# Perceiver block on one core: when GpSimd splits the queries' weights, and ScalarE's order beside it

## What is computed

```python
def _layernorm(x, axis=-1, eps=1e-05):
    m = jnp.mean(x, axis=axis, keepdims=True)
    v = jnp.var(x, axis=axis, keepdims=True)
    return (x - m) / jnp.sqrt(v + eps)
...
x = x + xattn(layernorm(x), ctx_768, w_q, w_k, w_v, w_o, b_o)     # x: 64*32 rows x 512
#   q = x @ w_q (512 x 1024), k = ctx @ w_k, v = ctx @ w_v, 16 heads of 64
#   softmax(q k' / 8) v, then @ w_o + b_o
x = x + attn(layernorm(x), w_attn, w_proj, decay_raw)              # 16 heads of 32, causal
x = x + ffn(layernorm(x), w1, b1, w2, b2)
```

## Time and profile before

| | us |
|---|---|
| median of 3 runs | 1648.69 |
| lowest, highest | 1645.7, 1652.7 |
| the profiled execution | 1647.76 |
| its span, first to last instruction | 1645.8 |
| TensorE busy | 1584.6 (96%) |
| VectorE busy | 1243.0 (76%) |
| ScalarE busy | 1035.2 (63%) |
| GpSimd busy | 786.4 (48%) |

### The profile page before, as it was taken

The page is one execution under the profiler, slowest core; times in us unless marked ns, Lnnn a source line. Parts: engine busy times, 40 slices in busy tenths (PEclk is TensorE's granted clock), DMA queues, the critical chain, the costliest instruction groups (busy, mean ns, idle before and its releaser), DMA issues. The chain is left out here.

```text
span 1645.8 us, 30117 instructions
## 1 busy us (share of the span) xinstructions
PE 1584.6 (96%) x11126; PEld 1384.3 (84%) x11126; DVE 1243.0 (76%) x2396; ACT 1035.2 (63%) x2050; POOL 786.4 (48%) x730
## 2 busy tenths in 40 slices
PE   6999999999999999999999999999997898999998
PEld 4888899998999999899998788998886677888886
DVE  5548878887887888788787774666666998879786
ACT  3338777777777777777776422444446666666665
POOL 3116546464554546555453241334435554656554
PEclk9999999999999999999999999999999999999999
DMA  9773434444343443534342862012132221010010
GB/s 267 216 246 99 124 110 105 128 108 130 96 120 112 108 132 94 144 93 117 114 133 83 290 211 71 21 59 76 55 104 85 69 60 57 26 49 23 7 52 26
DMA packets 173826, 173.63 MB, mean 105 GB/s; under 512 B 80944, under 2 KB 138352, under 8 KB 173680
## 3 DMA queue, kind: packets, MB, share of 16 engines
q1 hardware_dynamic: 173680, 171.71, 36.1%
HBM read 133.91 MB, written 37.75 MB: 104 GB/s over the span
## 5 line engine op out<-in xcount | busy, mean ns | idle before, releaser
L75 PE MATMUL p_bank_score<-p_ctxt,p_qo 128*128 128x256 f32 x2304 | 304.5, 286 | 1.0 <-ACT p_probs L997 0.7
L75 PEld LDWEIGHTS p_bank_score<-p_ctxt,p_qo 128*128 128x128 f32 x2304 | 288.1, 191 | 6.1 <-issue 2.4
L75 PE MATMUL p_bank_mix<-p_probt,p_ctx 128*128 128x512 f32 x1152 | 292.0, 397 | 0.5
L75 PEld LDWEIGHTS p_bank_mix<-p_probt,p_ctx 128*128 128x128 f32 x1152 | 207.4, 189 | 41.9 <-issue 3.8
L2017 PE MATMUL p_bank_down<-p_w,p_ht 128*128 128x512 f32 x768 | 190.0, 397 | 11.4 <-DVE p_ht L2113 6.8
L1194 DVE SCALAR_TENSOR_TENSOR p_qo<-p_bank_mix,p_odd,p_qo 128x512 fp32r<-128x512 f32 x192 | 143.8, 749 | 57.5 <-ACT p_qo L1011 49.8
L2017 PEld LDWEIGHTS p_bank_down<-p_w,p_ht 128*128 128x128 f32 x768 | 146.3, 191 | 46.5 <-issue 7.6
L1988 POOL TENSOR_TENSOR p_pieces<-p_pieces 128x512 f32<-128x512 f32 x64 | 110.3, 1723 | 154.2 <-ACT p_pieces L2059 154.2
L703 POOL TENSOR_TENSOR p_ctx<-p_ctx_in,p_ctx 128x768 fp32r<-128x768 f32 x64 | 118.5, 1851 | 131.7 <-ACT p_ctx L986 131.4
L1011 ACT ACTIVATE p_qo<-p_bank_mix,p_odd 128x512 fp32r<-128x512 f32 x192 | 132.4, 690 | 68.1 <-PE p_bank_mix L75 67.4
L997 ACT ACTIVATE p_probs<-p_bank_score,p_small 128x257 f32<-128x257 f32 x256 | 121.5, 476 | 58.8 <-DVE p_small L1175 55.2
(11 more groups left out here) (277 smaller groups left out, 3651.6 us busy)
## 6 DMA issues: line engine op xcount, KB each, us to landing
p_blocks_in<-in_ctx_dram SPq DMA_DIRECT2D x256, 96.0 KB, 2.4
p_ctx_in<-in_ctx_dram SPq DMA_DIRECT2D x64, 384.0 KB, 3.2
q<-p_ctx SPq DMA_DIRECT2D x64, 256.0 KB, 3.3
p_odd_in<-in_ctx_dram SPq DMA_DIRECT2D x64, 192.0 KB, 3.4
p_x<-in_x_dram SPq DMA_DIRECT2D x32, 256.0 KB, 4.3
p_quad<-q SPq DMA_DIRECT2D x32, 256.0 KB, 3.9
p_probt<-q SPq DMA_DIRECT2D x32, 256.0 KB, 4.2
p_o_in<-o SPq DMA_DIRECT2D x8, 1024.0 KB, 7.0
```

Source lines behind the costliest of these rows:

```text
L75: made = e.matmul(out, lhsT, rhs, start=n == 0, stop=n == last)
```

## The change

GpSimd gets a wait for `norm.chain` to reach NR, that is for the four tiles of the first group to be scaled, ahead of its first subtraction of weights. ScalarE copies weight blocks 0 and 1 before the four turned tiles, and blocks 2 and 3 behind them (before: 0, 1 and 2 before, 3 behind). No instruction is added beside the wait, and none is removed.

```diff
             make_identity(e, ident, ident_ready)
             e.memset(f32(none[:]), 0.0).then_inc(none_set, 1)
+            e.wait_ge(norm.chain, NR)
             for k in (0, 1, 3):
                 low_query_weights(k)
             for g in range(NQ):
@@
             norm.root(e)
-            for k in range(3):
+            for k in range(2):
                 high_query_weights(k)
             for i in range(NR):
                 norm.high(e, i, zts[0], i * P)
-            high_query_weights(3)
+            for k in range(2, KT):
+                high_query_weights(k)
             for g in range(NQ):
```

## The result

| | before | changed |
|---|---|---|
| median (20 runs each) | 1647.66 | 1651.38 |
| lowest, highest | 1644.2, 1652.7 | 1648.88, 1655.25 |
| ratio, 95% interval | | 1.0022 [1.0013, 1.003] |
| the profiled execution | 1647.76 | 1652.05 |
| its span | 1645.8 | 1649.9 |

The changed kernel is 0.22% slower, 3.7 us (2.1 to 4.9 by the interval): no change by the bound of 0.5% that the forecast used, and yet a loss that the runs show to be there. The forecast was 1652.0. The profiled execution is 4.3 us longer, its span 4.1.

A forecast was written before the change was run, and what follows sets the result against it. Start bound by the chain scale, turn, copy high (ACT), subtract low (DVE), four times. Sum: -3.5 (earlier products) +3.4 (value weights) +2.0 (stores, TensorE) +2.1 (clock) = +4.0 us on 1647.76, rounded to 1652; range 1645 to 1655.

The forecast's parts named there:

- (a): First four tiles: with POOL waiting, DVE scales each in about 0.54 us, the fourth from 10.8 to 11.35.
- The rival on the other side: Scaling not slow because of POOL: block 3 issued 6.1 us late, +7.7 us, 1655.5; chance 0.04.
- (b): Chain of turns, copies and subtractions behind the scaling: products start at 15.8 instead of 19.29, 3.5 us earlier.
- (c): ACT's copy of weight block 2 moves behind the four tiles and stays hidden: cost 0, slack 6 us.
- (d): POOL's first weight subtractions move from 9.0 to 11.4, done at 13.75 and 16.2; slack 2 and 5 us.
- (e): SP's queue: load of query block 3 issued at 13.8 instead of 11.4, everything behind it 2.4 us later.
- (f): Value weights land at 34.1; ACT waits there and the whole gain is spent, +3.4 us.
- (g): Stores of q land late: ACT copies tile 3 at 38.4 (+1.8 us), tile 4 at 40.2; 1.9 taken, bounds 0 to 2.1.
- (h): TensorE pauses 4.9 us before product 6, which starts 1.9 us later; lower clock costs 2.1 us, bounds 0 and 2.7.
- the gain is kept: Rival: transfers late by under 0.5 us, so -3.5 us or 1644.3; chance 0.19.
- The value weights alone: Rival: stores of q land in time, only value weights hold ACT; -0.3 to +1.8 us, 1647.5 to 1649.6; chance 0.21.
- it does nothing: Rival: both effects under 1 us, 1647 to 1649; chance 0.06.

The follow-up runs named there:

- e7: Changed kernel with GpSimd waiting for three scaled tiles instead of four; ratio 1.0008 [0.9998, 1.0018] against the kernel before.
- e1: Changed kernel with ScalarE's old order, so GpSimd's wait alone; ratio 1.0022 [1.0013, 1.0031] against the kernel before.
- e2: Kernel before with only ScalarE's new order of copies; ratio 1.0002 [0.9992, 1.0013] against the kernel before.
- e12: Kernel before with the load of query block 3 waiting for GpSimd's second subtraction instead of its first; ratio 1.0005 [0.9996, 1.0014].
- e5: Changed kernel with ScalarE's copies of the value weights behind products 5, 6, 7 instead of 1, 2, 3; ratio 1.0026 [1.0016, 1.0036] against before.
- e10: Changed kernel with a raw buffer of its own for query block 3, whose load waits for no subtraction; ratio 0.9992 [0.9982, 1.0002] against before.
- e3: Changed kernel with the load of query block 3 issued behind the keys' weights and x tiles 4 to 7; ratio 1.0014 [1.0005, 1.0023] against before.
- e8: Changed kernel with GpSimd waiting for one scaled tile instead of four; ratio 1.0008 [0.9997, 1.0019] against the kernel before.
- e6: Changed kernel with 20 extra matmuls, results unread, behind product 5 on TensorE; ratio 1.0016 [1.0006, 1.0025] against the kernel before.
- e9: Changed kernel with 30 extra matmuls, results unread, behind product 5 on TensorE; ratio 0.9998 [0.9989, 1.0007] against the kernel before.
- e11: Kernel before with a raw buffer of its own for query block 3; ratio 0.9997 [0.9988, 1.0006] against the kernel before.

## Why the prediction was right

By the steps of its sum:

- **(a)** held. Scaled tiles: 0.54 us each were predicted, three took 1.46 us and the fourth 0.55, ending at 11.38 (predicted 11.35). The rival on the other side, that the tiles are not slow because of POOL, is out; e7 turned the effect on again for one tile.
- **(b)** held: 15.65 against 15.8. No subtraction of the chain got slower beside POOL (0.69 us each).
- **(c)**, **(d)** held: block 2 was subtracted by 17.2, first wanted at 23.46; e1 and e2 show the order to be worth nothing. DVE's subtraction was there 0.28 us before POOL's ended (16.13) and took 1.37 us; without company it takes 1.22 (e1, at 16.25). The lock that the prediction weighed cost these 0.15 us and nothing behind them, as said; the last section shows that it is there.
- **(e)** held: issued at 13.85 (predicted 13.8), with 0.00 of the DMA engines busy from 12 to 14 us. Block 3 landed and was copied at 17.19 (landing predicted at about 17.2). The reading that the share before was 1.0 or more right behind the gap was too high for its first window, 12 to 14 us, which has 0.70, as the transfers start again in it; nothing hangs on it. e12, with this delay and nothing else, lost 2.6 us by its trace.
- **(f)** held in its effect, and was off by a little on the way: the delay reached the value weights' issue as 2.1 us, not 2.4 (27.91 against 25.78), and the first landed at 34.0 (predicted 34.1), since it took 6.1 us instead of 5.9. ACT stood there with its whole queue behind it.
- **(g)** held, and was the least certain step: copy of tile 3 at 38.60 (predicted 38.4), tile 4 at 40.21 (40.2). The bound of 0, stores that land in time, was wrong; e5 shows them to bind alone. The low part of tile 0 took 8.7 us behind the value weights instead of 3.7: it was issued earlier (29.81 against 32.32), as products came earlier, and landed 2.5 us later (38.5 against 36.0). The upper bound was close.
- **(h)** held in kind. The pause was 5.43 us (predicted 4.9), because product 5 ended at 36.8, half a microsecond before the 37.3 of the prediction. Product 6 started 2.5 us late, not 1.9: the turns 6 and 7 already ran at the lower clock (1.94 us instead of 1.03), which the prediction had counted behind product 6. By PE's stretch from these turns to product 7, the 4.30 us are 1.70 of later start and 2.60 of longer work; 0.21 of the latter also stand in kernels whose clock stayed at 1.00. So the low clock cost 2.4 us, where the prediction took 2.1, within its bound of 2.7. That 2.1 was a middle between two rows, and only one of them is shown to be the clock: the pause late in the trace (1.6 to 1.7 us, granted clock 0.50). The other, the first products of the kernel (2.5 us), ran at half rate while their windows show 1.00. That the middle came so near is in part luck; by the first row alone the sum would have been 3.5 to 3.6.
- The sum was 4.0; the trace has 4.3 at product 7 and at the end of the stage, the medians 3.7. The shift stayed a shift, as said.

Of the rivals, "the gain is kept" is out: product 6 came at 43.87, the share of the DMA engines was 1.01 or more in every window of 2 us from 16 to 36 us, and of the delay they caught up less than 0.4 us. e10 shows what it would have taken, an earlier issue, and that even then the gain of 3.5 us in front shrinks to 0.4 us, at the stores and at the clock. "The value weights alone" fell with e5, "it does nothing" with the interval [1.0013, 1.003].

What was not foreseen is how near the stores and the clock stand behind one another: of the experiments that were to beat before, e3 removed the idle gap and met a wait for block 3, and both e3 and e10 met the stores and the clock. What stays open: whether stores that land sooner would bring e10's lead through. It was not tried; it needs a fourth buffer for the parts of q, or stores issued from another queue.

## What to carry to other kernels

An engine that is made to wait at the start may free a buffer on which a whole DMA queue stands; look for who waits on its result there, and whether the DMA engines are idle behind that wait and full after it, since such a delay was hardly caught up here (2.5 us at the issue of block 3, 2.1 us 14 us later). A lead on TensorE was worth nothing here while the next transfer did not land sooner too, and a lead that ends in a pause can cost more than it was: where the clock fell to 1.2 GHz, the work behind takes 1.3 to 2.4 us longer. Moving a waiting load back in its queue put the backlog in front of it (e3); giving it a buffer of its own removed its wait (e10).

## What the runs showed of the hardware

- **VectorE and GpSimd hold each other up until the one that was first is done, where both of VectorE's inputs are in SBUF, or where it scales from SBUF to SBUF.** A scaled tile (128x512 float32 from SBUF to SBUF) took 0.55 us alone, and 2.63, 2.56 and (e7) 2.36 us beside a subtraction on POOL. In e7 the first of these began at 10.30 and, at half of 4.85 us each, ended near 12.7; the tile ended at 12.93. The kernel before has the opposite case, which was overlooked when it was read; DVE's block 2 and POOL's block 3:

```profile
19.15 1.22 DVE L1145 TENSOR_TENSOR p_wq<-p_raw,p_wq 128x1024 fp32r<-128x1024 f32 x1
```
```profile
19.53 3.06 POOL L678 TENSOR_TENSOR p_wq<-p_raw,p_wq 128x1024 fp32r<-128x1024 f32 x1 [5.70 <-ACT p_wq L962]
```

  DVE was first and took its 1.22 us, until 20.37; POOL came at 19.53 and took 3.06 instead of the 2.36 of the changed kernel's subtractions, so it lost 0.70 of the 0.84 us in which DVE was still at work. The Trainium skill (SBUF — State Buffer, section on the two separate sides) states it so: of a VectorE operation with two SBUF inputs or in a two-port mode, and a GpSimd operation, whichever starts first has the shared ports for its whole length. Where VectorE was first, these traces agree to within 0.14 us. Where GpSimd was first, the tiles ended 0.2 to 0.3 us behind the subtraction, sooner than the 0.55 us of a lone tile; so part of a tile's time is not held up. The subtractions with an input in PSUM, 0.69 us, were not touched.
- **A pause of about 2.2 us may or may not lower TensorE's clock.** After 2.18 us (e7), 1.92 (e12) and 1.84 (e8) it stayed at 1.00; after 2.17 (e10) and 2.18 (e6) it fell to 0.50, and so it did after 2.88 (e3), 5.43, 5.94 (e1) and 6.23 (e5). What product 6 took behind it differed from 3.00 to 4.79 us. So two executions with the same pause can differ by over 1.5 us. The timed runs fit with such falls making part of the spread: of the changed kernel's 20, the slowest (1655.25) has a mean granted clock of 0.985 and the quickest (1648.88) 0.992, and over all 20 time and clock have a correlation of -0.81. Where in the program the clock differed is not recorded.
- **The granted clock does not show the half rate of the program's first products.** Before, their 12 matmuls took 5.3 us and the next 12 2.8; in the changed kernel eight transposes at 9.71 took 1.94 us, as they did at 42.28 with 0.50. The windows at the start show 1.00. What slows them is not shown.
- **A store's landing goes by what stands before it in the queue.** The low part of q's first tile, 256 KB, took 3.7 us before, where it was issued 6.5 us behind the value weights (three loads of 512 KB). Issued 2.4 to 4 us behind them it took 6.6 to 7.4 (e3, e7, e8, e10, e12), issued 1.9 us behind them 8.5 to 9.7 (changed, e1, e5, e6, e9).
- **The same issues took different times.** L543's four merged issues took 5.13 us in the changed kernel, 6.32 in e5 and 6.45 in e8, which with L550 moved a landing by over 1 us; with the fourth buffer they took 6.73 (e10) and 2.63 (e11). What sets this stays open.
